# First layer's preparation rebuilt: diagonal taps on TensorE, offsets as rows, row and column tiles

## The reference, cut to what matters

```python
xn = _bn(x, bn1_g, bn1_b)
q = _gconv1x1(xn, qw)
qg = q.reshape(b * GROUPS, DH, H, W)
off = conv(qg, off_dw_w, stride 4, pad 1, 6x6 taps, feature_group_count=DH)   # depthwise, to 8 x 8
off = gelu(off + off_dw_b, approximate=False)
off = jnp.tanh(jnp.einsum('bchw,oc->bohw', off, off_pw_w)) * OFF_SCALE        # 2 channels: x and y
vx = gx[None] + off[:, 0];  vy = gy[None] + off[:, 1]
nx = 2.0 * vx / 7 - 1.0;    ny = 2.0 * vy / 7 - 1.0
kv = _grid_sample(xn, stack(nx, ny))            # bilinear: hat functions of the pixel distance in x and y
k = _gconv1x1(kv, kw);  v = _gconv1x1(kv, vw)
pos = grid_q[:, :, None, :] - grid_kv[:, None, :, :]
bias = jnp.sign(pos) * jnp.log1p(jnp.abs(pos))  # for every query, key and coordinate
bias = relu(bias @ cpb_w1 + cpb_b1)             # 2 -> 32
bias = relu(bias @ cpb_w2 + cpb_b2)             # 32 -> 32
bias = bias @ cpb_w3 + cpb_b3                   # 32 -> 1
sim = jnp.einsum('bhid,bhjd->bhij', qh, kh) + bias
```

## Time and profile before

| | |
|---|---|
| time before, median of 3 runs | 1797.34 us (1795.22 to 1797.75) |
| the profiled execution: time | 1797.25 us |
| its span in the profile | 1795.2 us |
| mean granted TensorE clock | 0.943 |
| busy over the whole span | PE 1536.4 us, DVE 919.5, ACT 861.5, POOL 297.7 |

### The profile page before, as it was taken

The page is one execution under the profiler, slowest core; times in us unless marked ns, Lnnn a source line. Parts: engine busy times, 40 slices in busy tenths (PEclk is TensorE's granted clock), DMA queues, the critical chain, the costliest instruction groups (busy, mean ns, idle before and its releaser), DMA issues. The chain is left out here.

```text
span 1795.2 us, 29725 instructions
## 1 busy us (share of the span) xinstructions
PE 1536.4 (86%) x12220; PEld 765.7 (43%) x12220; DVE 919.5 (51%) x1428; ACT 861.5 (48%) x1174; POOL 297.7 (17%) x126
## 2 busy tenths in 40 slices
PE   2689999999767997999999998999999999458598
PEld 1232222222233664666566665654444444226254
DVE  5658888888762544677776775010001000357242
ACT  2647777777533435677777764222222222230521
POOL 0036666666220001000000000000000000020000
PEclk7879999999998998899999999899999999879889
DMA  1000000000011003344343440000000000000000
GB/s 63 1 1 2 2 2 2 2 2 2 1 37 54 1 1 117 130 164 160 135 160 134 153 164 1 1 1 1 0 0 1 0 0 0 29 0 4 1 1 23
DMA packets 20657, 69.73 MB, mean 39 GB/s; under 512 B 688, under 2 KB 17072, under 8 KB 18096
## 3 DMA queue, kind: packets, MB, share of 16 engines
q1 hardware_dynamic: 20240, 66.86, 10.1%
q10 hardware_dynamic: 288, 1.05, 0.1%
HBM read 33.30 MB, written 34.60 MB: 38 GB/s over the span
## 5 line engine op out<-in xcount | busy, mean ns | idle before, releaser
L482 POOL TENSOR_TENSOR l_work<-l_a_scores,l_work 128x2048 f32<-128x2048 f32 x64 | 232.8, 3639 | 218.4 <-PE banks L599 116.9
L1769 PE MATMUL banks<-s_h,pack_l2f_l3f 128*128 128x512 f32 x512 | 221.0, 592 | 0.0
L1796 ACT ACTIVATE s_h<-banks,pack_l2f_l3f 128x512 f32<-128x512 f32 x128 | 87.9, 687 | 240.8 <-PE banks L1769 175.8
L540 DVE TENSOR_TENSOR l_work<-banks,sc_negc 128x1024 f32<-128x1024 f32 x128 | 156.4, 1222 | 49.5 <-PE banks L646 33.4
L502 ACT ACTIVATE l_work<-banks,pack_l 128x1024 f32<-128x1024 f32 x128 | 142.5, 1114 | 77.3 <-PE banks L599 76.4
L599 PE MATMUL banks<-l_work,pack_l 32*32 32x512 f32 x4096 | 159.9, 607 | 23.1 <-ACT l_work L502 19.4
L1362 PE MATMUL banks<-pack_l2a,r_e 128*128 128x128 f32 x1024 | 143.5, 283 | 26.1 <-ACT r_e L1414 26.1
L1449 DVE TENSOR_REDUCE r_raw<-banks 128x1 f32<-128x640 f32 (+1 forms) x128 | 109.5, 856 | 106.8 <-PE banks L1343 106.8
L1414 ACT ACTIVATE r_e<-banks,r_max 128x1024 f32<-128x1024 f32 x128 | 142.4, 1112 | 44.5 <-DVE r_max L1455 44.5
L1343 PE MATMUL banks<-r_k,r_q 32*128 32x128 f32 (+3 forms) x832 | 148.8, 466 | 1.1 <-DVE r_v L1287 1.1
L1769 PEld LDWEIGHTS banks<-s_h,pack_l2f_l3f 128*128 128x128 f32 x512 | 97.3, 190 | 122.5 <-issue 122.5
(11 more groups left out here) (374 smaller groups left out, 2157.7 us busy)
## 6 DMA issues: line engine op xcount, KB each, us to landing
distances<-r_rd SPq DMA_DIRECT2D x16, 2048.0 KB, 6.3
r_band<-distances SPq DMA_DIRECT2D x16, 1536.0 KB, 7.0
pack_l2f_l3f<-pack_dram_l2f SPq DMA_DIRECT2D x1, 2212.5 KB, 11.0
pack_l2f_l3f<-pack_dram_l3f SPq DMA_DIRECT2D x1, 1248.5 KB, 5.5
pack_l<-pack_dram_l SPq DMA_DIRECT2D x1, 1217.0 KB, 6.7
residual<-x ACTq DMA_DIRECT2D x2, 512.0 KB, 7.9
out<-residual SPq DMA_DIRECT2D x2, 512.0 KB, 3.1
pack_l2a<-pack_dram_l2a SPq DMA_DIRECT2D x1, 715.0 KB, 4.6
```

Of the source, the lines that this page charges most:

```text
L482: pool.tensor_tensor(image(H1R[:, c % 3]), bc(a, 2, 16), bc(b, 3, HW), ALU.add).then_inc(sem("added"), 1)
L540: dve.tensor_tensor(image(H2M[:, (2 * c + part) % 3]), image(PS[:, MAX + j:MAX + j + 2]), bc(NEGC[:, j:j + 2, n, i, rows(half)], 3, HW), A ...
L1769: ins = pe.matmul(bank, W["w2"][:, col:col + P], H1[:, c, m], start=(m == 0), stop=(m == HB - 1))
```

## The change

The preparation `l0_prepare` is rewritten, with three edits outside it (the weight pack, the size of `NF`, its reading in `negb`). In order:

- Image 1 is normalised by ScalarE. VectorE builds `TAP`, 36 diagonal matrices of 128 x 128 from the identity and the tap weights, in two operations. It also takes over the four copies into `Q`, and these follow the copies into `qpad`.
- The convolution is 36 products on TensorE that accumulate in one bank, with `qpad` read at a stride of 4 as the moving operand. They stand ahead of the 16 transposes.
- The offsets are held as rows: row 32(2c + b) + 4g + t for coordinate c, image b, group g and quarter t of the keys, four equal rows for each offset. Four products of 64 columns in column tiles make them; tanh, coordinates and pixels are operations of 64 columns.
- For the hats the pixels are spread to all partitions by products with ones: VectorE masks `px` to `spread` (512 columns), and four products in row tiles write two banks for x and two for y. ScalarE reads the hats' input from these banks.
- GpSimd multiplies the hats to `wt`. `F` and `NF` are one operation each. `layer1(u)` takes image `u % 2` and group `u // 2`, its two products stand in two row tiles of 32 partitions and write the bank pair of their image. Sampling runs in four column tiles of 32 channels and 128 columns each, so only pairs of groups are computed, and the masking is two operations of 128 columns.
- `a_out` moves to VectorE but for six units (3, 7, 11, 13, 14, 15) that stay on ScalarE. TensorE's order is `layer1` 0 to 3, `sample(0)`, then two units before each `sample(c)` up to `c` = 5, `sample(6)`, `sample(7)`, k and v, `layer1` 14 and 15, the transposes.
- `negb` reads `NF` and `cpb_w1` in a row tile of 32 partitions.

```diff
-    p.add("off_pw", np.repeat(np.tile(L("off_pw_w").T, (HEADS, 1))[:, :, None], P, axis=2))
+    pw = np.zeros((HEADS, DH, 2, HEADS, 4), np.float32)
+    for g in range(HEADS):
+        pw[g, :, :, g] = L("off_pw_w").T[:, :, None]
+    p.add("off_pw", pw.reshape(P, 2 * HEADS * 4))
...
+    p.add("first", ((rows[:, None] % 32) == 4 * np.arange(HEADS)).astype(np.float32))
+    p.add("tmask", (rows[:, None] % 4 == np.arange(4)).astype(np.float32))
+    p.add("pmask", (rows[:, None] // DH % 2 == np.arange(2)).astype(np.float32))
...
         @block.gpsimd
         def _(pool):
             pool.memset(qpad[:], 0.0).then_inc(sem("border"), 1)
+            pool.memset(ones[:], 1.0).then_inc(sem("ones"), 1)
+            pool.wait_ge(sem("hx"), 1)
+            for c in range(8):
+                pool.wait_ge(sem("hy"), c + 1)
+                if c >= 2:
+                    pool.wait_ge(sem("sampled"), c - 1)
+                pool.tensor_tensor(wt[:, c % 2], hx[:], hy[:, c % 2], ALU.mult).then_inc(sem("wt"), 1)
...
+            for h in range(2):
+                t = slice(h * TAPS // 2, (h + 1) * TAPS // 2)
+                dve.tensor_tensor(TAP[:, t], bc(W["ident"], 1, TAPS // 2), bc(W["off_dw_w"][:, t], 2, P), ALU.mult
+                                  ).then_inc(sem("taps"), 1)
+            for n in range(NCH):
+                dve.wait_ge(sem("q_in"), n + 1)
+                dve.tensor_copy(Q[:, n * CH:(n + 1) * CH], PS[:, n]).then_inc(sem("q_flat"), 1)
...
+            link(dve.scalar_tensor_tensor(V[:], V[:], 4.0, W["kgrid"], ALU.mult, ALU.add))
             link(dve.tensor_scalar(V[:], V[:], 2.0 / 7.0, -1.0, ALU.mult, ALU.add))
+            link(dve.tensor_scalar(px[:], V[:], 1.0, HW / 2.0, ALU.add, ALU.mult))
+            dve.tensor_tensor(spread[:], bc(px[:], 1, HEADS), bc(W["first"], 2, KEYS), ALU.mult).then_inc(sem("spread"), 1)
...
+            dve.tensor_tensor(F[:], sgn[:], mag[:], ALU.mult).then_inc(sem("f"), 1)
+            dve.scalar_tensor_tensor(NF[:], sgn[:], -1.0, mag[:], ALU.mult, ALU.mult)
...
+            for u in range(UNITS - 2):
+                if u not in A_ON_ACT:
+                    a_out(u)
+                b_out(u)
             dve.wait_ge(sem("sampled"), 8)
+            got = PS[:, SAMPLE:SAMPLE + NB, 0:P].rearrange("p b (g k) -> p b g k", g=2)
+            link(dve.tensor_scalar(kv[:], got[:, :, 0], W["pmask"][:, 0:1], None, ALU.mult))
+            dve.scalar_tensor_tensor(kv[:], got[:, :, 1], W["pmask"][:, 1:2], kv[:], ALU.mult, ALU.add).then_inc(sem("kv"), 1)
...
             for c in range(8):
+                hat(c)
+                if c in (1, 3, 5):
+                    a_out(2 * c + 1)
+            a_out(13)
+            a_out(14)
...
+            pe.wait_ge(sem("q_in"), NCH)
+            for t in range(TAPS):
+                ky, kx = divmod(t, 6)
+                if t % (TAPS // 2) == 0:
+                    pe.wait_ge(sem("taps"), t // (TAPS // 2) + 1)
+                ins = pe.matmul(PS[:, CONV, 0:NB * KEYS], TAP[:, t], qpad[:, :, ky:ky + 29:4, kx:kx + 29:4],
+                                start=(t == 0), stop=(t == TAPS - 1))
+            ins.then_inc(sem("conv"), 1)
+            pe.wait_ge(sem("off"), 1)
+            for c in range(2):
+                for b in range(NB):
+                    r = 32 * (NB * c + b)
+                    ins = pe.matmul(PS[r:r + 32, ZED, 0:KEYS], W["off_pw"][:, 32 * c:32 * c + 32], off[:, b], start=True,
+                                    stop=True, tile_position=(0, r), skip_group_check=True)
+            ins.then_inc(sem("shift"), 1)
...
+                    ins = pe.matmul(PS[:, (GRID_Y if c else GRID_X) + b], ones[r:r + 32],
+                                    spread[r:r + 32].rearrange("p g k -> p (g k)"), start=True, stop=True,
+                                    tile_position=(r, 0))
+            ins.then_inc(sem("grid"), 1)
+
+            def layer1(u):
...
+                    ins = pe.matmul(PS[:, 2 * b + c], W["cpb_w1"][r:r + 32, g * P:(g + 1) * P], F[r:r + 32], start=True,
+                                    stop=True, tile_position=(r, 0))
...
             def sample(c):
                 pe.wait_ge(sem("wt"), c + 1)
                 for b in range(NB):
+                    for q in range(PAIRS):
+                        r = 32 * q
+                        ins = pe.matmul(PS[r:r + 32, SAMPLE + b, 0:P], XT[:, b * 8 + c, r:r + 32],
+                                        wt[:, c % 2, b * CH + q * P:b * CH + (q + 1) * P], start=(c == 0), stop=(c == 7),
+                                        tile_position=(0, r), skip_group_check=True)
...
+                    ins = pe.matmul(PS[:, NEGB, low * 256:low * 256 + 256], W["cpb_w1"][r:r + 32, k * P:(k + 1) * P],
+                                    NF[r:r + 32].rearrange("p (k y) -> p k y", y=HW)[:, :, rows(half)], start=True,
+                                    stop=True, tile_position=(r, 0), skip_group_check=True)
```

More of the change, by code:

```diff
@@ L230, in _ @@
             link(dve.tensor_scalar(s1[:], W["bn1_g"], BN_SCALE, None, ALU.mult))
[L231 to L249, removed]
@@ L389, in _ @@
                     ins.then_inc(sem("xt"), 1)
-            pe.wait_ge(sem("offm"), 1)
+            pe.wait_ge(sem("ones"), 1)
+            pe.wait_ge(sem("spread"), 1)
+            pe.wait_ge(sem("tanh"), 1)
             for c in range(2):
                 for b in range(NB):
-                    ins = pe.matmul(PS[:, 4 + 2 * c + b], W["off_pw"][:, c * P:(c + 1) * P],
-                                    offm[:, b].rearrange("p g k -> p (g k)"), start=True, stop=True)
-            ins.then_inc(sem("shift"), 1)
-            pe.wait_ge(sem("xt_out"), 4)
-            pe.wait_ge(sem("tanh"), 1)
+                    r = 32 * (NB * c + b)
+                    ins = pe.matmul(PS[:, (GRID_Y if c else GRID_X) + b], ones[r:r + 32],
[3 more added lines that the diff above has]
+            def layer1(u):
+                b, g = unit(u)
+                if u == 0:
+                    pe.wait_ge(sem("f"), 1)
+                    pe.wait_ge(sem("xt_out"), 4)
+                if u >= 2:
+                    mine = u - 2 in A_ON_ACT
+                    pe.wait_ge(sem("a_act" if mine else "a_dve"), a_done(u - 2, mine))
+                    pe.wait_ge(sem("b_out"), u - 1)
+                for c in range(2):
+                    r = 32 * (NB * c + b)
+                    ins = pe.matmul(PS[:, 2 * b + c], W["cpb_w1"][r:r + 32, g * P:(g + 1) * P], F[r:r + 32], start=True,
+                                    stop=True, tile_position=(r, 0))
+                ins.then_inc(sem("ab"), 1)
             def sample(c):
@@ L432, in _ @@
             for n in range(NB * PAIRS):
[L433 removed]
+                ins = pe.transpose(PS[:, GRID_Y + n // 4, (n % 4) * P:(n % 4 + 1) * P],
                                    vm[:, n // 4, 2 * (n % 4):2 * (n % 4) + 2].rearrange("p g k -> p (g k)"), W["ident"])
@@ L436, in _ @@
                     ins.then_inc(sem("vt"), 1)
-            for n in range(12, NB * HEADS):
-                layer1(n)
 def reg_wait(eng, sem, value, passed):
```

203 lines of the change are left out of this document (82 added, 121 removed).

## The result

| | before | after |
|---|---|---|
| median in this comparison | 1797.17 us (1795.22 to 1797.75) | 1772.14 us (1770.72 to 1775.4) |
| profiled execution | 1797.25 us | 1775.4 us |
| its span | 1795.2 us | 1773.6 us |
| end of the preparation | 108.2 us | 84.4 us |
| first instruction of the scores | 111.3 us | 88.0 us |

The ratio is 0.9865 (0.9848 to 0.9882). The change saves 25 us where 44.4 was forecast. The windows of after, cut at the ends of its own steps, show where the shortfall lies.

The account below looks back on a forecast made before the run. The preparation was taken as a serial pipeline bound by whichever engine works in each stretch. Ending it at 63.8 us instead of 108.2 gains 44.4: span 1795.2 - 44.4 = 1750.8, plus 2.05 around it, 1753 us; range 1746 to 1766.

Parts of the forecast that it names:

- The start: Preparation up to the last copy into the padded image: still ends at 16.7 us, zero change, +-0.5.
- The convolution's term: 36 TensorE products replace VectorE's 21.5 us stretch: 8.1 us plus 0.3 handing over, gelu at 25.1 instead of 38.2.
- rival A: Convolution products take twice 0.224 us, at half clock or (second form) by their strided read: +8, 1761 us; chance 0.11.
- Offsets, pixels, hats and logarithm: Between gelu and loop: offsets done at 26.6 us, x hats start at 29.45, Ln and table end at 34.85.
- ScalarE now sets the pace: Loop: ScalarE's hats and copies take 19.7 us, to 54.55; GpSimd's last product ends at 56.75; TensorE and VectorE below.
- Rival B: Loop not ScalarE's: TensorE at 1.2 GHz with units one behind the other, +11, or GpSimd at 2.59, +1; 1760; chance 0.13.
- Rival D: Row tiles do not run side by side at full precision; the loop is TensorE's, 1764 us; chance 0.04.
- the bounds: GpSimd's weight product of 1024 columns in the loop: 2.2 us taken, bounds 1.82 and 2.59.
- The tail: Last sampling to last A copy: 6.0 us, plus 1.0 for half clock; preparation ends at 63.8 us instead of 108.2.
- After it: Score stage and later stages: unchanged, 0, at best 3 us less; old stages merely earlier.
- Rival C: Score stage stays at lower clock: small form 1756 to 1764, chance 0.05; beyond 18 cycles, slower than before, chance 0.03.

Follow-up runs that it names:

- e1: After with the padded image stored by column phase, so that each convolution tap reads adjacent floats: 1764.72 us, ratio 0.983.
- e2_stride2: After with the convolution reading every second float instead of every fourth (wrong pixels): one execution, 1760.29 us.
- e5: After with GpSimd multiplying only 128 of 1024 columns of each weight product (wrong values): one execution, 1769.32 us.
- e6: After with VectorE's copies of A covering only 64 of 512 columns (wrong bias): one execution, 1766.37 us.
- e4: After with useless TensorE products, ten before unit 0 and one each round, each restarting the sampling sums: 1764.74 us, ratio 0.9828.
- e7: After with phase-stored padded image, units 14 and 15 before the last two samplings, and dummy products (start flag only in the first): 1756.49 us, ratio 0.9789.
- e3_tail: After with layer-1 units 14 and 15 before the last two samplings and their copies ahead of the k and v masks: 1768.24 us, ratio 0.9842.

## Why the prediction was wrong, step by step

*The start* was late by 0.75 us: the last q copy ends at 17.45, not 16.7. The eight q records stand 0.85 us apart, from 10.13 to 16.8, while image 0 was ready 0.35 earlier than before. In before the last of them stood 0.43 us apart, since the clock had risen by then. When it rises differs from one execution to the next with the same q products: they take 6.68 us here, 5.55 in before, and 5.2 to 6.8 in the experiments. Image 1 was normalised by 12.4, not 10.5, because ScalarE waited for x until 9.87; it was still in time.

*The convolution's term is the first that failed*, +8.6 us: from the last q copy to gelu 8.4 forecast (8.1 and 0.3 of handing over), 17.0 measured. The prediction took L1041's rate, which is for contiguous columns, and let VectorE's taps speak against a penalty for the stride. The clock was as forecast: 1.00 in the window, and the weight loads beside the products take 0.21 us, near the 0.19 of e1 and not the 0.34 that q's take at the lower level. e1_phases and e2_stride2 showed the stride alone to be the cause, which is rival A in its second form. The Trainium skill (Advanced Engine Details and Errata, SBUF Cachelines) asks for at least two accesses to each 16-byte line; this case agrees in the main for TensorE: two of four floats cost 0.137 us a record against 0.121, one of four 0.235. What VectorE's row shows, 0.32 us for 64 columns with the same stride, says nothing of TensorE. It was also misread: the 0.34 us for 64 contiguous columns was extrapolated, and after's L260, the same kind of operation on 64 adjacent columns with a constant factor, takes 0.23. How much of the difference is the stride and how much the factor read for each partition, no run separates.

*Offsets, pixels, hats and logarithm* together took 0.8 us less than forecast (1.03 for offsets where 1.5 stood; the pixels 2.76 against 2.85, with all four grid products in 1.14 us; x hats to Ln 5.18 against 5.4).

*The loop's step, "ScalarE now sets the pace", is the second that failed*, +8.75 us: 30.65 us from the end of Ln to the last GpSimd product, 21.9 forecast. The prediction added up each engine's work a round, TensorE's at the upper clock, and took the largest sum. It passed over the dependence that two bank pairs make: a unit's products, its two copies on VectorE behind the two of its neighbour, and the next unit in the same bank. e5 and e6 show it to be this chain (GpSimd made short: first period unchanged; VectorE's copies made short: 0.94 less), e4 and e7 that TensorE's clock is inside it: 7.9 us at 1.2 GHz, 6.2 at 2.4 GHz, a dummy product included. From the end of Ln to the last GpSimd product e7 takes 25.8 us, so about 4.9 of the 8.75 go with the lower clock and 3.9 are left with the clock at 0.99. Rival B named the clock, and gave 1760 with it. Its picture of units one behind the other for want of tiles was wrong, since four tiles do work side by side; units 2 and 3 come apart because VectorE frees their banks one after the other. Rival D fell with the same rows. GpSimd's 2.33 us were within the bounds.

*The tail is the third*, +3.35 us: 7.05 forecast with the clock's part, 10.4 measured. It lists the work in order but misses that `b_out(14)` stands before the masked copies on VectorE. e3_tail shows the new order to be worth 4.0 us, 2.6 of them this wait. The new kernel's code had the order in it.

*After it*, the score stage kept all of the gain: it began 23.3 us earlier and ended 24.5 us earlier. Rival C did not occur: from the stage's start to the steady stretch the clock was 0.65 over 23.5 us, in before 0.57 over 25.8. Later 2.9 us are lost again, not in one place: `l0_attend` begins 24.4 us earlier and `l0_mlp` 22.9; the heads of L2 begin 22.0 earlier and end 23.9 earlier; the last stage begins 21.6 earlier. The cause is not shown. The executions of after differ among themselves by more (4.7 us), and this one is the slowest.

Together: 0.75 + 8.6 - 0.8 + 8.75 + 3.35 = 20.65 us, which is 84.4 - 63.8 but for rounding. In the median the miss is 19.1 us (1772.1 against 1753). The range reached to 1766 since each of the rivals was priced alone; A and B came together, and with the tail.

The steps above are from the profiled execution of after, which is 3.3 us over the median.

## What to carry to other kernels

Before a strided view becomes TensorE's moving operand, store it so that the columns of a product are adjacent floats; the copy that writes it is the place for the stride. Where a loop alternates over two bank pairs, add up the way of one bank (product, copies queued ahead of its own, next product) at both levels of the clock, not only the work of each engine. Products without use held the clock up here, but each one inside the loop also stands in the path (0.63 us here). When an operation is moved behind another on TensorE, look through the queues of the engines that read it for what now stands ahead of the urgent work.

## What the runs showed of the hardware

- A product of 128 float32 columns (two records) takes 0.24 us with adjacent floats (e1), 0.27 with every second (e2) and 0.47 with every fourth (after), at a granted clock of 1.00.
- TensorE was busy 23.9 of 30.0 us in the loop and got 0.61 of its clock; with dummy products it was busy 25.5 of 31.0 us and got 0.99, from an upper level that had been held by ten such products while it would have rested.
- Four row tiles of 32 x 128 with 512 float32 columns each take 1.14 us together at 2.4 GHz and 2.09 at 1.2 GHz; at 1.2 GHz one unit of two tiles alone takes as long (unit 2 from 47.80 to VectorE's next copy at 49.91).
- GpSimd multiplies two plain operands of 1024 columns in 2.33 us, 2.3 ns a column; L482 adds 2048 columns, both operands with repeated ones, in 3.64, 1.8 ns a column.
- A product with a start flag in columns 256 to 511 of a bank restarts the sums that other products build in columns 0 to 127 of it: with the flag in every dummy (e4) the network's output is off by a relative 0.08, with it in the first alone, before the sums begin (e7), it is not.
